# Tile 0 of a nearest-row search in a written-out order, x in three parts, the context in eight loads

## The reference, cut to what matters

```python
qp     = einsum('bld,ed->ble', layernorm(x), Wq)      # 1024 x 128
scores = einsum('bld,bmd->blm', qp, kv)               # 1024 x 6404
idx    = argmax(scores, axis=-1)
mem    = kv[idx]                                      # 1024 x 128
...
x = x + tanh(g_xattn) * attention(qp, mem)            # 16 heads of 8
x = x + tanh(g_ffn) * mixture_of_experts(layernorm(x))  # router, top 2 of 8, capacity 160
```

## Time and profile before

| what | value |
|---|---|
| runs of the kernel before | 321.02, 323.48, 325.03 us; median 323.48 |
| span of the profiled execution | 321.0 us |
| PE busy | 282.7 us, 88% of the span |
| DVE busy | 199.6 us, 62% |
| ACT busy | 157.5 us, 49% |
| POOL busy | 88.0 us, 27% |

### The profile page before, as it was taken

How to read it: one execution, slowest core, us unless ns; L and a number is a source line. 1 busy time by engine, 2 the same in 40 slices (tenths; PEclk the granted TensorE clock), 3 DMA queues, 4 the chain that set the end, 5 groups by cost and what they waited for, 6 DMA issues and landing times.

```text
span 321.0 us, 5442 instructions
## 1 busy us (share of the span) xinstructions
PE 282.7 (88%) x1821; PEld 221.1 (69%) x1821; DVE 199.6 (62%) x700; ACT 157.5 (49%) x337; POOL 88.0 (27%) x175
## 2 busy tenths in 40 slices
PE   4999999999898778869999899799799987978993
PEld 2688999999787235548677677575486753468993
DVE  4585556765898777887878787611543508534344
ACT  1575555454444014757776676679525320055630
POOL 3874155454654522005600000100024000344000
PEclk9999999999999987997999999999999999799998
DMA  7822456656200000019081000000001000011002
GB/s 218 277 103 106 165 192 213 203 179 224 89 23 17 16 8 20 1 51 366 20 228 37 6 0 3 24 16 2 0 3 38 3 0 0 16 35 26 10 0 67
DMA packets 18460, 24.11 MB, mean 75 GB/s; under 512 B 2120, under 2 KB 14986, under 8 KB 18426
## 3 DMA queue, kind: packets, MB, share of 16 engines
q1 hardware_dynamic: 16836, 20.39, 18.9%
q0 software_dynamic: 1184, 3.14, 4.1%
q10 hardware_dynamic: 406, 0.16, 0.2%
HBM read 12.62 MB, written 10.93 MB: 73 GB/s over the span
## 4 chain that ended last, share of the span: by engine, by line
PE 57%; DVE 17%; issue 9%; DMA 7%; ACT 5%; POOL 4%; SPq 0%; DVEq 0%; ACTq 0%; POOLq 0%
PE ps L1554 7%; PE ps L1599 6%; PE ps L1586 4%; PE ps L1434 4%; DVE mx L1154 3%; PE ps L1436 3%; PE ps L1435 3%; PE ps L1736 3%; DMA pair<-in_ctx_dram,at 3%; PE ps L1742 3%; PE ps L1765 3%; PE ps L1494 2%; PE ps L1495 2%; DVE kv_nat L1145 2%; DMA kv_nat<-in_ctx_dram 2%
## 5 line engine op out<-in xcount | busy, mean ns | idle before, releaser
L1434 PE MATMUL ps<-shared,q_hi 128*128 128x400 f32 (+1 forms) x128 | 46.6, 364 | 1.8 <-DVE best L974 0.9
L734 ACT ACTIVATE gain<-ps 128x400 f32<-128x400 f32 (+1 forms) x64 | 32.3, 505 | 31.5 <-PE ps L1436 31.1
L1154 DVE TENSOR_REDUCE mx<-ps 128x1 f32<-128x384 f32 x84 | 41.1, 548 | 9.9 <-PE ps L1586 9.8
L974 DVE CUSTOM_DVE_ANT_0 kv_nat<-ps,gain 128x400 f32<-128x400 f32 (+1 forms) x64 | 35.9, 571 | 17.2 <-PE ps L1436 14.7
L1435 PE MATMUL ps<-shared,q_hi 128*128 128x400 f32 (+1 forms) x128 | 44.3, 346 | 0.0
L1436 PE MATMUL ps<-shared,q_lo 128*128 128x400 f32 (+1 forms) x128 | 44.2, 345 | 0.0
L840 ACT ACTIVATE kv_nat<-ps 128x512 f32<-128x512 f32 x72 | 39.5, 605 | 9.0 <-PE ps L1599 8.3
L1599 PE MATMUL ps<-q_rows,k_blk 128*128 128x256 f32 x192 | 39.9, 303 | 2.1 <-DVE mx L1145 1.7
L1599 PEld LDWEIGHTS ps<-q_rows,k_blk 128*128 128x128 f32 x192 | 32.2, 196 | 6.7 <-issue 3.3
L1586 PE MATMUL ps<-k_blk,q_rows 128*128 128x384 f32 x84 | 29.0, 372 | 1.5 <-DVE mx L1154 1.4
L1434 PEld LDWEIGHTS ps<-shared,q_hi 128*128 128x128 f32 x128 | 24.1, 188 | 4.1 <-DVE best L974 2.1
(11 more groups left out here) (314 smaller groups left out, 556.8 us busy)
## 6 DMA issues: line engine op xcount, KB each, us to landing
m_rows<-kv_nat SPq DMA_DIRECT2D x48, 201.0 KB, 2.1
kv_nat<-in_ctx_dram SPq DMA_DIRECT2D x5, 640.0 KB, 9.7
ew_sb<-in_L_ffn_eW_dram SPq DMA_DIRECT2D x1, 2048.0 KB, 10.2
rw_sb<-in_L_ffn_rW_dram SPq DMA_DIRECT2D x1, 1024.0 KB, 5.7
x_sb<-in_x_dram SPq DMA_DIRECT2D x2, 256.0 KB, 3.7
xn_rows<-xn SPq DMA_DIRECT2D x2, 256.0 KB, 2.3
out_dram<-fin SPq DMA_DIRECT2D x4, 128.0 KB, 1.8
rw_sb<-in_L_ffn_rW_dram SPq DMA_DIRECT2D x1, 256.0 KB, 2.8
```

What stands on the lines that cost most here:

```text
L734: act.activation(gain[:, m % 3, 0:end - start], ps[:, b:b + end - start], ACT.Relu).then_inc(s_rl, 1)
L974: dve.tensor_tensor_reduce(out=m_all[b2][:, start:end], in0=ps[:, b:b + end - start], in1=gain[:, m % 3, 0:end - start], scale=1.0, scalar ...
L1154: dve.tensor_reduce(to, sc, AX.X, ALU.max).then_inc(s_p1u, 1)
L1434: pe.matmul(o, q_h, hi, start=True, stop=False)
```

## The change

- SP loads x in three parts, tile 0, tiles 1 to 3, tiles 4 to 7, and the context in eight pieces of 2, 2, 4, 4, 4, 4, 5 and 1 tiles, in the order x0, pieces 0 to 3, x1, pieces 4 to 7, x2. The nine small operands (all but Wq) are issued by SP behind these; before, ACT issued them at the start.
- Statistics, normalising, turning, projecting and splitting go by these three parts. Part 0 goes ahead of S0, part 1 inside tile 0, part 2 in tile 1: statistics of x2 at the end of tile 0 on DVE, normalised after chunk 1, turned on PE after chunk 2, projected after chunk 4, split in chunk 5, behind `find_in_chunk(0)`.
- Tile 0 has an order written out, the same list for PE, ACT and DVE.
- In tile 0 the chunks use two pairs of PSUM banks (0 to 3), so chunk m waits for chunk m-2; banks 4 and 5 hold parts 0 and 1 of the projection. From tile 1 on there are three pairs as before.
- One of the three matmuls on `ones` at L1373 stays.

```diff
-        KV_PIECE = 5
-        q_bank = (4, 6)
+        PIECES = [(0, 2), (2, 4), (4, 8), (8, 12), (12, 16), (16, 20), (20, NKV - 1), (NKV - 1, NKV)]
+        Q_PARTS = [(0, 1), (1, 4), (4, NT)]
+        q_bank = (4, 5, 6)
+        def banks_of(m):
+            return m % 2 if m < NCH else (m - NCH + 2) % 3
+        def banks_free(m):
+            return m - 1 if m < NCH else m - 2
...
-        def turns_at(c):
-            upto = [4, 6, 8, 10, 11, 13, 2 * NKG, 2 * NKG]
-            return range(upto[c - 1], upto[c])
+        TURN, TURN_X, PROJECT, SCORE = range(4)
+        FIRST_TILE = ((TURN, 0), (TURN_X, 0), (TURN, 1), (PROJECT, 0), (TURN, 2), (SCORE, 0), (TURN, 3), (TURN, 4), (SCORE, 1),
+                      (TURN, 5), (TURN, 6), (SCORE, 2), (TURN, 7), (TURN, 8), (SCORE, 3), (TURN_X, 1), (TURN, 9), (SCORE, 4),
+                      (TURN, 10), (PROJECT, 1), (SCORE, 5), (TURN, 11), (TURN, 12), (SCORE, 6), (TURN, 13), (SCORE, 7))
...
         # SP
+            load_x(0)
+            for j in range(4):
+                load_kv(j)
+            load_x(1)
+            for j in range(4, 7):
+                load_kv(j)
...
+            load_x(2)
+            sp.dma_start(wkv_nat[:], Wkv).then_inc(s_small, 16)
...
         # POOL
-            for half in range(NL):
-                pool.wait_ge(s_ve, half + 1)
...
-            for j in range(6):
+            rstd_of(0)
+            for j, (a, b) in enumerate(PIECES):
                 pool.wait_ge(s_kv[j], 16)
...
+                if j == 4:
+                    rstd_of(1)
...
             pool.memset(v_ext[:], 0.0)
+            rstd_of(2)
...
         # ACT
-            act.dma_start(wkv_nat[:], Wkv).then_inc(s_small, 16)
...
-            round_kv([0])
-            copy_turned(0)
-            round_kv([1])
-            round_q(0)
-            round_kv([2, 3])
+            for what, n in FIRST_TILE:
+                if what == TURN:
+                    round_kv([n])
+                elif what == TURN_X:
+                    copy_turned(n)
+                elif what == PROJECT:
+                    round_q(n)
+                else:
+                    gains_of(0, n)
...
         # DVE
+            spread_of(0)
+            normalise(x_sb, range(*Q_PARTS[0]), 1)
...
+                    for what, k in FIRST_TILE:
+                        if what == TURN:
+                            kvt_lows([k])
+                            if k == 5:
+                                spread_of(1)
+                            elif k == 8:
+                                normalise(x_sb, range(*Q_PARTS[1]), 2)
+                        elif what == PROJECT:
+                            low_q(k)
+                        elif what == SCORE:
+                            sums_of(0, k)
+                    spread_of(2)
...
-                    if i == 0 and c == 5:
-                        normalise(x_sb, range(4, NT), 2)
-                    if i == 1 and c == 4:
-                        low_q(1)
+                    if i == 1 and c == 1:
+                        normalise(x_sb, range(*Q_PARTS[2]), 3)
+                    if i == 1 and c == 5:
+                        low_q(2)
...
         # PE
-            for _ in range(3):
-                pe.matmul(bank(7), ones[:], ones[:].unsqueeze(1).broadcast_to([P, 4, P]), start=True, stop=True)
-            turn_kv([0])
-            turn_x(0)
-            turn_kv([1])
-            pe.wait_ge(s_cs, 1)
-            project_q(0)
-            turn_kv([2, 3])
+            pe.matmul(bank(7), ones[:], ones[:].unsqueeze(1).broadcast_to([P, 4, P]), start=True, stop=True)
...
+            for what, n in FIRST_TILE:
+                if what == TURN:
+                    turn_kv([n])
+                elif what == TURN_X:
+                    turn_x(n)
+                elif what == PROJECT:
+                    if n == 0:
+                        pe.wait_ge(s_cs, 1)
+                    project_q(n)
+                else:
+                    pe.wait_ge(s_klo, turned_by(n))
+                    scores(0, n)
...
-                    if i == 1 and c == 0:
+                    if i == 1 and c == 2:
                         pe.wait_ge(s_qn, 1)
-                        turn_x(1)
-                    if i == 1 and c == 3:
-                        project_q(1)
+                        turn_x(2)
+                    if i == 1 and c == 4:
+                        project_q(2)
                     if i == 1 and c == 6:
                         project_q_nat(1)
```

More of the change, by code:

```diff
@@ L275, in program @@
         router_parts = fin[:].rearrange("p t d -> p (t d)")
-        s_x = [sem(f"x_loaded{half}") for half in range(NL)]; s_kv = [sem(f"kv_loaded{j}") for j in range(6)]
+        s_x = [sem(f"x_loaded{part}") for part in range(3)]; s_kv = [sem(f"kv_loaded{j}") for j in range(8)]
         s_small = sem("small_loaded"); s_wql = sem("wq_loaded"); s_w = sem("weights_loaded")
@@ L900, in _, with spread_of @@
             link(dve.memset(best[:], LOWEST))
-            for half in range(NL):
-                dve.wait_ge(s_x[half], 16)
-                for i in range(4 * half, 4 * half + 4):
+            def spread_of(part):
+                a, b = Q_PARTS[part]
+                dve.wait_ge(s_x[part], 16)
+                for i in range(a, b):
                     n[0] += 1
@@ L910, in _ @@
                 dve.wait_ge(s_dve, n[0])
-                t = slice(4 * half, 4 * half + 4)
-                dve.tensor_scalar(var_eps[:, t], mv[:, t, 1], EPS, None, ALU.add).then_inc(s_ve, 1)
-            normalise(x_sb, range(4), 1)
+                dve.tensor_scalar(var_eps[:, a:b], mv[:, a:b, 1], EPS, None, ALU.add).then_inc(s_ve, 1)
+            spread_of(0)
+            normalise(x_sb, range(*Q_PARTS[0]), 1)
             def kvt_lows(jobs):
@@ L921, in kvt_lows, with low_q @@
                                       kvt_hi[part][:, cols], ALU.subtract).then_inc(s_klo, 1)
[L923 to L931, removed]
+            def low_q(part):
+                dve.wait_ge(s_qhi, part + 1)
+                dve.tensor_tensor(q_lo[:, q_cols(part)], in_q_bank(part), q_hi[:, q_cols(part)], ALU.subtract
+                                  ).then_inc(s_qlo, 1)
             def dot_of(i):
@@ L970, in _ @@
                         dve.wait_ge(s_at, i - 1)
[L971 to L976, removed]
+                    sums_of(i, c)
                     if c == 2 and i >= 2:
@@ L1186, in attention_dve @@
                         if period == NQ and s == 1:
-                            normalise(x1, range(4), NL + 1)
+                            normalise(x1, range(4), len(Q_PARTS) + 1)
                         if period == NQ + 1 and s == 0:
@@ L1196, in _ @@
             by_count(dve, attention_dve)
-            normalise(x1, range(4, NT), NL + 2)
+            normalise(x1, range(4, NT), len(Q_PARTS) + 2)
             low_xn(1)
@@ new lines, in _ @@
+            for what, n in FIRST_TILE:
[10 more added lines that the diff above has]
+                    scores(0, n)
+            project_q_nat(0)
+            small_operands()
+            for i in range(1, NT):
+                for c in range(NCH):
+                    if i == 1 + Q_PARTS[1][1] - 1 and c == 0:
+                        pe.wait_ge(s_qlo, 3)
+                    scores(i, c)
+                    if c == 2:
```

196 lines of the change are left out of this document (103 added, 93 removed).

## The result

The changed kernel takes 328.6 us (median; 326.14 to 333.71) against 324.31 us for the kernel before beside it (321.02 to 327.07). The ratio is 1.0166, 95% interval 1.014 to 1.0192: slower, clear of the scatter, but by less than 2%. Each ratio here leaves out executions more than 1.5% above their kernel's fastest, so it needn't be the quotient of the two medians (here 1.0132). The forecast was 329.0.

What follows compares the result with a forecast made beforehand. The prediction took PE in its program order as the bound through the search. Its terms, -3.55 + 6.9 + 2.0 = +5.35 us, on the median of 323.48 gave 328.8, forecast as 329, range 327 to 331.

Steps and rivals of the forecast that it cites:

- The head: Opening up to S0: less data to land first, so S0 starts at about 9.9 us, 3.55 us sooner than 13.45.
- The raise of one column: POOL's raise for x tile 0 in the opening, costed at 1.04 us, the only row, measured for four columns.
- the landing of piece 1: Opening: context piece 1 lands at about 6.8 us, then POOL makes its difference by 7.55, ahead of job 1.
- The order of tile 0: S0 to S8: PE waits for low halves of jobs placed right behind chunks; 6.9 us longer, bounds 5 and 8.
- a cycle of 3.20: Tile 0: a chunk's 1.18 us plus 2.02 us for the turning job that the next chunk waits for.
- Tile 1: From S8: PE waits 0.6 us for normalised x2 and about 1.4 for low_q(2); together 2.0 us, bounds 0.5 and 3.
- From S7 to S8 nothing changes: 3.02: End of tile 0: the stretch from S7 to S8 keeps its 3.02 us from before the change.
- The second rival: Clock stays low past S0 with fewer opening matmuls on ones: 1.2 to 2.9 us more, 330.8 us; chance 0.22.
- The first rival: Tile 0 stays packed, tile 1's waits don't show, only S0 moves the end: -3.55, 319.9 us; chance 0.10.

Runs made afterwards that it cites:

- e1: The changed kernel with only tile 0's written order altered, every turning job one chunk earlier; 323.95 us, ratio 0.9988 to the kernel before.
- e2: The kernel before with only its turning jobs moved one chunk later, as the change places them; 331.7 us, ratio 1.0219.
- e3: The kernel before with two pairs of PSUM banks instead of three in tile 0, nothing else; 324.51 us, ratio 0.9972.
- e4: The changed kernel with tile 1 reordered: low_q(2) ahead of find_in_chunk(0), x2's turning and project_q_nat(1) one chunk later; 328.04 us, ratio 1.0105.
- e5: The changed kernel with a matmul on ones filling PE's waits ahead of S1, S2, S3, S6 and S7; 326.0 us, ratio 1.0071.
- e7: The changed kernel with e1's and e4's edits, x1's statistics and normalising moved on DVE and its raise on POOL; 322.68 us, ratio 0.9963.
- e8: The changed kernel itself, unaltered, measured and profiled once more; 329.53 us, ratio 1.0148 to the kernel before.

## Why the prediction was right, and where it wasn't

It forecast 329.0, with -3.55 + 6.9 + 2.0; the measured places are -4.40, +7.11 and +1.41, +1.85, about nothing in the rest. Point by point:

- **The head** gained 0.85 us more than forecast: S0 at 9.05, not 9.9, just outside the bounds 9.2 to 12. Two terms were too large. The raise of one column took 0.58 us, not the 1.04 of the only row, and pieces 0 and 1 were in earlier than 6.8, as the timelines of POOL and DVE after the change show (differences 0 and 1 are done at 5.90):

```profile
3.94 0.58 POOL L538 TENSOR_TENSOR rstd<-var_eps,minus_half 128x1 f32<-128x1 f32 x1 [1.85 <-DVE var_eps L952]
4.50 1.40 POOL L545 TENSOR_TENSOR kv_nat<-kv_nat 128x256 f32<-128x256 f32 x2
...
8.62 0.28 DVE L968 TENSOR_TENSOR q_lo<-ps,q_hi 128x128 fp32r<-128x128 f32 x1
```

  So the path was another, too: the prediction has S0 set by the landing of piece 1 and its difference, and they didn't set it. The chain that ended last runs on PE itself from 3.29 us to S0, without a wait of more than 0.11 us:

```profile
3.73 1.71 PE ps L1426 x2
5.44 0.85 PE ps L1399 x4
...
6.51 0.85 PE ps L1399 x4
7.36 0.63 PE ps L1413 x2
...
8.02 0.92 PE ps L1399 x4
```

  A job's four turns hold it for 0.85 us here, against 0.45 in tile 0: PE is at its lower level, which the prediction expected in jobs 0 and 1 but counted as small. Job 2 is over at 8.94 and `q_lo` at 8.90, and S0 follows both.
- **The order of tile 0** was right in mechanism and size: a cycle of 3.20 forecast and 3.20 measured, S0 to S7 20.15 forecast and 20.41 measured. Inside it two errors nearly cancel: `turn_x(1)` waited 1.02 us instead of 0.4, so that S4 came 0.5 late, and S4 to S5 took 1.97 us instead of 2.4. e1 (the order put back: 4.9 of the 7.11 us go) and e2 (the order alone: +6.0 from S0 to S7) show that the written order is the cause of 5 to 6 us; what is left in e1 stands beside x1's work in tile 0 and a wait of 0.48 us for POOL. e3 shows that the two pairs of banks cost nothing, as costed.
- **Tile 1** was right: 2.0 forecast, 1.85 measured, with two waits for the two reasons given, and e4 takes the loss away by exactly those edits. The waits were forecast at 0.6 and 1.4 us and read 0.33 and 1.04; a record of 0.34 us outlasts its share of PE (0.18) by some 0.16, so by the starts they cost about 0.5 and 1.2.
- **"From S7 to S8 nothing changes: 3.02"** is the step that failed. It took 4.36, as PE ran S7 and `project_q_nat(0)` at the lower of its levels. The second rival had this mechanism, but at S0 and with the few records on ones as its reason; in the profiled execution the records of S0 were already those of the higher level, and the clock fell at 29.1 us, behind the 1.14 us that PE waited ahead of S6 and within the 0.72 ahead of S7. e2 has the same fall without any of the opening's edits, and e5 is without it once PE is busy in the waits. The Trainium skill tells, in "TensorE: Matmul & The Clock Gate", A second HAM failure mode: psum-queue depth-cycling, of a kernel whose short idle times between groups of matmuls came so often that the clock went to and fro between its two levels. By that rule such waits cost more than their own length, and the trace agrees: 1.41 us on top of them here, with one fall instead of many. e4, which has the same opening and whose S0 ran at the lower level (S0 to S1 4.62 us instead of 3.18), shows that the rival as written also happens, in some executions.
- **The size of the total** is better than its terms, and that is luck: the head missed by -0.85, S0 to S7 by +0.26, S7 to S8 by +1.4, tile 1 by -0.15, and what lies behind S16 by -0.5, which adds up to less than +0.2. One execution of each kernel gives these 5.5 us, and executions of one kernel lie 6 us and more apart; by the medians of all runs the loss is 4.3.
- **The first rival**, that the head's gain carries through, falls even with the order put back alone; in e7, with tile 1 and x1 mended as well, 2.61 us of it reach S16. The four cases side by side, by the start of S16: old opening and old order 41.20, new opening and old order (e1) 41.49, old opening and new order (e2) 49.15, both new 47.17. Of the head's 4.40 us e1 spends 0.7 on job 3 ahead of S0, 2.2 on x1's work in tile 0, and 1.9 in tile 1.

## What to carry to other kernels

Where one engine is the bound and its work passes through others and back, write its order so that each piece has a whole unit of other work between the pass and the return; here one place in a list cost 5 to 6 us and swallowed the 4.4 us of a shorter opening. Count every such return as a wait of the handoff's full length (2.02 us here, less what stands between), and count the clock with it: idle time on TensorE in the middle of dense work can cost more than its own length. Then compare several executions before giving a later stretch the blame for a gain that doesn't reach the end: of 2.6 us won at S16 1.7 were gone at S63, but the same stretch differed by 1.2 us between two executions of one kernel.

## What was not expected of the hardware

- The granted clock fell to half from 29.1 to 32.5 us, after waits that left PE busy 10.75 of 14.70 us, not after one long pause. The low stretch came at different places in different executions: at 29 to 33 us after the change and in e8, at 33 to 36 in e2, in the opening and again at 23 to 26 in e4; between S1 and S63 not at all in e5, nor in the seven others without such waits.
- The granted clock's column read 1.00 at 8 to 10 us of e4, while the records of S0 there were 0.54 us long, as at a granted clock of 0.50 later on. In the opening the lengths of the records are the better witness, as with the matmuls on ones.
- POOL's raise took 0.58 us for one column and 1.04 for four.
